# The hand-over at the end of a feed-forward: a block's sum and norm on VectorE ahead of the last block's residual, all low parts last, idle transposes moved

## The reference, cut to what matters

```python
# end of _L1_xattn_ref: xt is the running value of the block
h = layernorm(xt, g_ffn, b_ffn)
h = jax.nn.gelu(h @ W1 + b1, approximate=False) @ W2 + b2
xt = xt + h
return layernorm(xt, g_norm_out, b_norm_out)
...
x = x + _L1_xattn_ref(_layernorm(x, axis=-1), ...)
x = x + _L1_attn_ref(_layernorm(x, axis=-1), ...)
```

## Time and profile before

| | |
|---|---|
| median of 3 runs | 1803.25 us (1791.06 to 1805.01) |
| the profiled execution's own time | 1802.59 us |
| its span, first to last instruction | 1800.8 us |
| TensorE busy, share of the span | 93% |
| VectorE, ScalarE, GpSimd busy | 55%, 33%, 20% |
| mean granted TensorE clock | 0.949 of full |
| TensorE's last `down` product ends | 1277.01 us |
| the self attention's first product begins | 1301.74 us |

### The profile page before, as it was taken

One profiled execution on the slowest core, in us unless ns is written; L12 is line 12 of the kernel. 1 busy time (PEld: TensorE's weight loads), 2 busy tenths in 40 slices (PEclk: granted clock), 3 DMA queues, 4 the chain that ended last, 5 costly groups with the idle time before them and its releaser, 6 DMA issues. The chain is left out here.

```text
span 1800.8 us, 23403 instructions
## 1 busy us (share of the span) xinstructions
PE 1675.6 (93%) x8886; PEld 1304.1 (72%) x8886; DVE 993.6 (55%) x1525; ACT 595.0 (33%) x1085; POOL 359.1 (20%) x327
## 2 busy tenths in 40 slices
PE   7799999999998989998999998989599899999996
PEld 4799999999995777864565656668486666676772
DVE  1569678687684634456999996653525630000014
ACT  4353454444521211103544432154245521111110
POOL 0521331233121020011554542300200010000010
PEclk9899999999999989998998988989798989999998
DMA  4322131323113567548163552220001097696860
GB/s 132 110 78 88 56 110 61 98 62 111 55 42 124 193 251 267 183 147 295 60 228 115 174 212 94 94 112 1 18 32 48 12 325 262 220 337 228 301 221 30
DMA packets 113044, 251.45 MB, mean 140 GB/s; under 512 B 14726, under 2 KB 44438, under 8 KB 108182
## 3 DMA queue, kind: packets, MB, share of 16 engines
q1 hardware_dynamic: 104352, 230.72, 36.8%
q10 hardware_dynamic: 6006, 10.62, 1.7%
q0 software_dynamic: 2560, 8.39, 1.4%
HBM read 230.95 MB, written 18.75 MB: 139 GB/s over the span
## 5 line engine op out<-in xcount | busy, mean ns | idle before, releaser
L415 PE MATMUL x_s_ps<-x_cxt,x_qs 128*128 128x400 f32 (+1 forms) x1152 | 246.1, 359 | 9.5 <-POOL x_qs L388 5.5
L1204 PEld LDWEIGHTS e_ps<-e_xg,e_w 128*128 128x128 f32 x1792 | 209.8, 195 | 35.7 <-issue 35.5
L441 PE MATMUL x_o_ps<-x_cx,x_pt 128*128 128x386 f32 (+1 forms) x1248 | 230.3, 343 | 0.0
L441 PEld LDWEIGHTS x_o_ps<-x_cx,x_pt 128*128 128x128 f32 (+1 forms) x1248 | 220.6, 190 | 1.4
L1204 PE MATMUL e_ps<-e_xg,e_w 128*128 128x128 f32 x1792 | 212.8, 279 | 9.0 <-issue 6.1
L415 PEld LDWEIGHTS x_s_ps<-x_cxt,x_qs 128*128 128x128 f32 x1152 | 207.3, 192 | 10.8 <-issue 10.6
L1196 PE MATMUL e_ps<-e_w,xt 128*128 128x512 f32 x352 | 163.2, 606 | 3.7 <-DMA e_w<-in_L_ffn_W 3.7
L2398 PE MATMUL x_s_ps<-x_cxt,x_qs 128*128 128x512 f32 (+1 forms) x384 | 140.7, 523 | 2.8 <-ACT x_sc L2519 1.7
L1443 DVE TENSOR_TENSOR e_y<-e_ps,e_b 128x512 f32<-128x512 f32 x20 | 13.7, 687 | 210.2 <-PE e_ps L1196 210.2
L491 DVE TENSOR_TENSOR x_pt<-x_t_ps,x_pt 128x512 fp32r<-128x512 f32 (+1 forms) x128 | 74.7, 586 | 92.3 <-ACT x_pt L581 92.1
L2398 PEld LDWEIGHTS x_s_ps<-x_cxt,x_qs 128*128 128x128 f32 x384 | 67.9, 194 | 79.3 <-issue 78.5
(11 more groups left out here) (437 smaller groups left out, 2736.6 us busy)
## 6 DMA issues: line engine op xcount, KB each, us to landing
e_w<-in_L_ffn_W SPq DMA_DIRECT2D x16, 4096.0 KB, 16.5
x_cxt<-in_ctxT SPq DMA_DIRECT2D x8, 2401.5 KB, 8.8
x_cx<-in_ctx SPq DMA_DIRECT2D x8, 2304.0 KB
e_w<-in_L_ffn_gate_up_proj SPq DMA_DIRECT2D x8, 2048.0 KB, 8.5
x_stage<-in_ctxT SPq DMA_DIRECT2D x16, 768.0 KB, 4.4
x_stage<-in_ctx SPq DMA_DIRECT2D x16, 768.0 KB, 6.2
e_w<-in_L_ffn_down_proj SPq DMA_DIRECT2D x8, 1024.0 KB, 9.4
x<-in_ctxT SPq DMA_DIRECT2D x8, 768.0 KB, 4.4
```

Of the source, the lines that this page charges most:

```text
L415: last = nc.tensor.matmul(s_ps[:, n, 0:b - a], qs[:, u % 2, p, c, :], cxt[:, q, c, a:b], start=(m + c == 0), stop=(m + c == len(PARTS) + C ...
L441: last = nc.tensor.matmul(o_ps[:, 0:WIDE], pt[0:rows, p, t, :], cx[0:rows, q, t, :], start=(t + m == 0), stop=(t + m == KT - 1 + len(PARTS ...
L1204: last = nc.tensor.matmul(u_ps[:, g % 2, a * PER + n, :], w1[:, e % PAIR, m, a * hidden + c * P:a * hidden + (c + 1) * P], xg[:, m, :], st ...
```

## The change

VectorE's order is changed: block t + 1's sum and norm stand ahead of block t's residual, and all four low parts come after the last block's residual. The rows of the last block's second norm are made by VectorE (`scaled`, L165 after) in place of ScalarE, after a wait for three blocks' transposes; GpSimd's product for that block is left out. The 14 idle transposes stand ahead of block 1's and of block 2's transposes, and no longer ahead of block 3's.

```diff
@@ gpsimd
                     following.deviation(pool, t)
-                    following.shifts(pool, t)
+                    if t + 1 < TT:
+                        following.shifts(pool, t)
@@ tensor
                 for t in range(TT):
-                    for n in range(IDLE):
-                        if t == TT - 1:
-                            nc.tensor.transpose(ps[:, u_bank, (n % KC) * P:(n % KC + 1) * P], ident[:, :], ident[:, :])
+                    for n in range(IDLE if 0 < t < TT - 1 else 0):
+                        nc.tensor.transpose(ps[:, u_bank, (n % KC) * P:(n % KC + 1) * P], ident[:, :], ident[:, :])
                     turn_next(t)
@@ scalar
                 for t in range(TT):
-                    following.act_rows(act, t)
+                    if t + 1 < TT:
+                        following.act_rows(act, t)
                     act.wait_ge(turn_ready, t + 1)
@@ vector
                 block_out(0)
-                block_next(0)
                 for t in range(1, TT):
                     block_out(t)
-                    block_next(t)
-                    next_low(t - 1)
-                next_low(TT - 1)
+                    block_next(t - 1)
+                block_next(TT - 1)
+                next_low(0)
+                next_low(1)
+                dve.wait_ge(turn_ready, TT - 1)
+                following.scaled(dve, TT - 1)
+                for t in range(2, TT):
+                    next_low(t)
```

## The result

| | before | after |
|---|---|---|
| median, 9 runs each | 1793.47 us (1786.05 to 1805.01) | 1779.12 us (1772.78 to 1787.43) |
| ratio, with its 95% interval | | 0.9931 [0.9902, 0.9961] |
| same kernels timed again later | 1792.26 us, 16 runs | 1783.38 us, 12 runs: 0.9927 [0.9900, 0.9954] |
| profiled execution, own time and span | 1802.59, 1800.8 | 1779.03, 1777.2 |

Faster by 0.7%, some 12.5 us, within 1% as forecast. One of the 12 later runs, the profiled one, was a disturbed execution of 2435 us; it is left out of the ratio and its trace isn't used. The two profiled spans are 23.6 us apart, and the first thing to see is that this isn't all the change's: VectorE's first sum of the tail, ahead of which nothing was changed, stands at 1268.93 before and at 1258.93 after, 10.0 us earlier.

What follows compares the result with a forecast made beforehand. TensorE was taken to bound the program, but the tail to be a chain of waits between engines. Terms 9.1 + 1.9 = 11.0 us took 1802.59 to 1791.6, put at 1791.8 us, range 1781 to 1798.

Steps and rivals of the forecast that it cites:

- The reading of the bound: Tail: no engine full, a chain between engines; VectorE waits 10.2 us for ScalarE's copies while the next block's sum stands behind.
- VectorE's new line: VectorE's reordered sums, norms and residuals in the tail: last statistics finished at 1285.23 instead of 1294.37, 9.1 us earlier.
- Block 2's hand-over: From block 2's second statistics to its transposes: L143 held until 1284.3, rows at 1286.2, transposes done at 1287.35.
- Block 3's hand-over: From last statistics to the self attention's first product: 5.5 us instead of 7.4, a 1.9 us share of the gain.
- the clock's case: TensorE's clock kept as before: low for both last hand-overs and for 5.9 us of the self attention.
- Rival A: TensorE's clock stays up or returns earlier through the moved idle transposes: gain 12.5 to 14.9 us, chance 20%.
- the forecast's own case: Tail and its seam to the self attention: gain 9 to 12.5 us, chance 68%.
- GpSimd's time: Block 3's inverse deviation, held by L3238 and L3244, ready at 1283.4 to 1283.8, wanted at 1283.54: cost 0, up to 0.3.
- Rival B: GpSimd kept out over several VectorE instructions, so inverse deviations come late: gain only 5.5 us, 1797, chance 9%.
- The 0.6: Possible loss of 0.6 us if block 2's L154 waits behind low part 0 on VectorE; taken as 0.
- C: Self attention's first products stay at low clock, 40 us more than now: 9 us slower, 1811, chance 2%.
- The cover of the idle transposes: None of the 28 idle transposes ahead of blocks 1 and 2 delays anything, though by only 0.1 us at block 2.

Runs made afterwards that it cites:

- after again: The changed kernel unaltered, profiled in another execution: tail 21.76 us, first copy 27.25 us, own time 1783.80 us.
- own signal: Against the changed kernel, a separate semaphore for the last block's rows, without the wait for block 2's transposes: tail 20.50 us, own time 1793.07 us.
- the product taken from PSUM: Against the kernel before, L3238 reads the product's PSUM bank in place of y, same instruction form: tail 30.43 us.
- one-operand tensor_scalar: Against the kernel before, L3238 without the product by the norm's gain, one SBUF operand instead of two: tail 31.92 us.
- before again: The kernel before unaltered, profiled in another execution: tail 31.71 us, first copy 34.75 us, own time 1787.86 us.

## Why the prediction was right, point by point

**The reading of the bound** held. VectorE's line, in which a low part waited for ScalarE with the next block's sum behind it, was what cost: the order alone takes 9.7 of the 11.8 us (8.6 of 10.7 against the second trace of before).

**VectorE's new line** (9.1 us) came within 0.12 us: last statistics 9.26 us earlier, against the first trace of before; against the second, in which GpSimd was held less, it is 8.7. **Block 2's hand-over**, with the hold on L143 by the last residual, came to 0.1 us.

**Block 3's hand-over** (1.9 us) was right at low clock: without idle transposes the tail is 21.74, and after again 21.76, where 21.83 was forecast. In the first trace it is 0.8 us less by the clock. The weak step was the choice of the clock's case: "low for both last hand-overs and for 5.9 us of the next stage". In six executions with after's order and rows it fell ahead of block 2's transposes in two (after again, no idle), inside block 3's in two (after, own signal), and in the two with more idle transposes not at all; and even before's 5.9 us weren't before's own, as the second trace has 0. Rival A was neither right nor wrong: the clock stayed up for most of the tail, worth 0.8, but not into the self attention, and the first trace's 12.1 at the first copy lies in the forecast's own case.

**GpSimd's time**, put at 0 to 0.3: 0. L143 of block 3 took 0.22 us beside L3239, not the hold that was forecast, and the inverse deviation was there at 1272.33, 1.1 us before the residual wanted it. The prediction read L143's hold as certain wherever L3238 runs; by all traces it is not. For block 0 the room was also read too wide, 3.9 us: from the end of its L3239 to its residual the prediction's own times give 2.5, and after has 2.6, which was enough. Rival B didn't occur. **The 0.6** for the low parts was 0: L143 and L145 took 0.22 and 0.57 us at 1275.33 and 1275.63, with low parts, which read PSUM, under way from 1275.03 to 1276.28, and L154 0.27 us at 1274.98. By the rule of the Trainium skill, "SBUF — State Buffer", section "Who interferes with whom", that was to be expected, and these rows agree, as do L143 and L145 beside the product taken from PSUM (0.22 and 0.57). The one-operand tensor_scalar held L143 for 0.50 us; the same section lets tensor_scalar into modes that use both ports, and no run here tells whether that was the cause.

**C** didn't occur: the longest low stretch at the self attention's start was 5.9 us, in before itself, and 5.6 behind the new order.

**The cover of the idle transposes** was wider than forecast: 14 took 1.69 us at full clock, and block 2's stood 2.2 us clear of them.

**The time**: in the tail 10.0 to 11.8 us less over the four traces, where 11.0 was forecast; in whole times 11.0 us, 0.61%, was forecast and 0.69% [0.39, 0.98] measured. The absolute 1791.8 was 12.7 too high, and 1779.12 is 1.9 below the range's low end: before's median of three, 1803.25, was itself 9.8 above that of nine. So most of the error is in the base; the other 2.9 us are less than the interval's half width, and no term is shown wrong by them.

## What to carry to other kernels

When an engine's order is written by hand, look for an instruction that waits for another engine's answer while work that is long ready stands behind it, and put that work in between; here that was 8.6 to 9.7 us without removing a single instruction. A change of a fraction of a per cent is read from marks inside the trace, counted from the last instruction ahead of it, not from spans: equal code ahead of this one ended anywhere within 23 us. Idle transposes pay where TensorE's clock is up at the seam (2.1 us here at the first copy, 26.22 to 24.11 and 25.65 to 23.50, one execution of each) and cost where they stand between ready rows and their transposes (1.2 us with the order alone, 1.45 in before). Both can hold of the same ones: those 14 ahead of block 3's cost 1.2 us in the tail and mostly had the clock back for the next stage, so moving them away brought nothing at the first copy. Follow such a change past the seam.

## What the runs showed of the hardware

- Who is held when GpSimd's small instructions meet VectorE's product of two large SBUF operands isn't settled by the order of their starts in the trace. The product always starts 0.04 to 0.06 us ahead of L143. Either L143 then takes 0.78 us and L145 comes only behind the product, or L143 takes 0.22, the product 0.77 or 0.78 instead of 0.75, and L145 0.85. With the new order blocks 0 and 1 are of the first kind and blocks 2 and 3 of the second in all seven traces; with the old order all four blocks are of the first kind in one trace, two in two, three in one. GpSimd's idle time ahead of it doesn't decide either: 4.98 us in block 3 of before (0.78) and 4.99 in before again (0.22). What decides is open.
- The granted clock falls and rises at places that shift by us between executions of one kernel: down 17.1 or 18.9 us from the first sum in after, back before or 5.9 us behind the self attention's start in before. In before it alone is some 3.0 of 3.55 us at one seam.
